# Moving five pieces of the shared network out of the expert loop, and a new order at the end of a mixture-of-experts kernel

## The chip, the cores and the metric

The kernel runs on one core of a Trainium2 chip. The metric is the time of one execution in microseconds (us); three runs of the kernel before are given, and their median counts. One further execution was taken by the hardware profiler, and every row shown here comes from it.

## The reference

The layer takes `x` (4, 512, 512) and `ctx` (4, 512, 128). First comes a graph attention of two layers. Its mask is the layernorm of `x`, multiplied by 1e10, so each row attends to one node alone: the kernel takes the position of each row's largest value instead of a softmax. Then a mixture of experts runs on the layernorm of the sum:

```python
x = x + xattn(ctx, layernorm(x), W0, ..., W1, ...)         # rows picked by argmax, twice
xf = layernorm(x).reshape(2048, 512)
scores = softmax(xf @ gate_w.T); topk_w, topk_idx = top_k(scores, 6)   # 64 experts, 128 rows each
gx = xp[buf_tok]                                            # (64, 128, 512), gathered
g, u = split(einsum('ech,ehi->eci', gx, gate_up_proj))      # 192 + 192
eo = einsum('eci,eih->ech', silu(g) * u, down_proj) * buf_w
routed = zeros.at[buf_tok].add(eo)                          # scattered with an addition
shared = silu(xf @ sh_gate.T) * (xf @ sh_up.T) @ sh_down.T  # 512 -> 384 -> 512, every row
out = x + routed + shared
```

All matrices are float32. The 2048 rows are 16 tiles of 128 rows (`NT`), in 4 groups of 4 tiles (`B`, `TB`).

## The kernel before, in words

Each engine has its own written-out queue (`block.sync`, `gpsimd`, `tensor`, `scalar`, `vector`), and semaphores join them. There are four stages.

**Attention**, up to about 95 us of the span. It fills `k.x`, one 128x512 tile per 128 rows.

**Routing**, up to about 154 us. TensorE makes the gate's logits (`gate`, `turn_logits`), VectorE picks the six experts (`choose`), TensorE counts places (`place`), VectorE makes one-hot matrices of the places (`split_high`, `split_low`, `split_rest`), TensorE turns them into lists of rows (`invert`, `collect`), and VectorE writes the list of each expert into `table` (L1283). GpSimd's gathers need this table. Four groups go through these steps one after the other.

**The expert loop** over `e` = 0 to 63. SyncE loads an expert's weights: `gu_w` (six buffers, `U`) for each expert, `dn_w` for each pair. GpSimd gathers the expert's rows into `gx`. TensorE transposes them (L811), multiplies by `gu_w` (L852), turns the hidden rows (L818) and, for pairs of experts, multiplies by `dn_w` (L827, L834, L837). ScalarE copies and takes silu, VectorE multiplies and writes `y` (L1337, eight buffers, `YB`), two experts at a time behind each odd `e`. GpSimd then scatters `y` with an addition into one of two sums in HBM, the lanes (L547): lane 0 is `out`, lane 1 is `odd_sum`. Within a lane each scatter waits until the one before has landed (`added`). Experts alternate between the lanes, except that the last `LAST` = 6 (58 to 63) all go to lane 0.

**Shared units** are woven in. The shared network is cut into 40 units, ten for each group of four tiles. The first six are `half_up` (L711, eight matmul records, 128x512; gate and up side of three slices `s` in turn), the last four are `shared_down` (L722, six records, one tile each). A `half_up` pair needs ScalarE's `silu` and VectorE's `shared_up` (L1214), and a `shared_down` VectorE's `shared_down` (L1220, adds to `k.x`, counts `x3_ready`). Units 0 to 4 (`EARLY` = 5) are in the routing stage, 32 to 39 (`LATE` = 8) behind the loop. The 27 between are spread by

```python
def first_unit(e):
    return EARLY + min(e * (units * B - EARLY - LATE) // (E - 2), units * B - EARLY - LATE)
```

**The end.** SyncE reads the two sums back by group (`load_sum(j, b)`, 1 MB each; lane 1 goes into the free `xnT` and, for the last group, into `y`; lane 0 into the free `gu_w`). VectorE adds them to `k.x` in `merge(j, b)` (L1370, four adds of one tile). SyncE stores each group when its tiles are complete (`store_out`, L352). `judge` computes a flag from bounds. After the block every engine loads the flag (`nc.values_load`) and, only if it is set, a general path would run; with these inputs it doesn't. `sent` is a semaphore which GpSimd raises behind the issue of scatters 62 and 63; VectorE waits for it before `merge(1, 0)` and before `shared_up(last, 1)`. SyncE's last instruction in the block waits for all stores (`out_stored`), ahead of the load of the flag.

Of the kernel before, what the change touches and what calls it, by code (L numbers as in the profile page):

```python
# [39 lines left out]
U = 6  # L40
# [3 lines left out]
LAST = 6  # L44
EARLY = 5
LATE = 8
# [29 lines left out]
def allocate(nc, ctx, k):  # L76
    def sb(name, shape, dt=F32):
        return ctx.enter_context(nc.sbuf_tensor(name, shape, dt))

    k.x = sb("x", [P, NT, D])  # L80
    k.ident = sb("ident", [P, P])
    k.ones = sb("ones", [P, P])
    k.flag = sb("flag", [1, 1], I32)
    k.gateT = sb("gateT", [P, KC, E])
    k.upT = sb("upT", [P, KC, 2 * SI])
    k.downT = sb("downT", [P, SC, D])
    k.mhalf = sb("mhalf", [P, NT])
    k.mv = sb("mv", [P, NT, 2])
    k.rstd = sb("rstd", [P, NT])
    k.tri = sb("tri", [P, P], F16)  # L90
    k.eighth = sb("eighth", [P, P], F16)
    k.strict = sb("strict", [P, P], F16)
    k.upto = sb("upto", [P, P], F16)
    k.pick_a = sb("pick_a", [P, (2 * SLO - 1) * SHI], F16)
    k.pick_z = sb("pick_z", [P, (2 * SLO - 1) * SHI], F16)
    k.same_e = sb("same_e", [P, 8])
    k.digit = sb("digit", [P, SHI], F16)
    k.token = sb("token", [P, NT])
    k.psum = [ctx.enter_context(nc.psum_tensor(f"bank{i}", [P, 512], F32)) for i in range(8)]


def main_block(nc, k, a):
# [3 lines left out]
    with ExitStack() as ctx:  # L106
# [140 lines left out]
        merged, total_ready, out_stored = (sem(s) for s in ("merged", "total_ready", "out_stored"))  # L247
# [46 lines left out]
        def first_unit(e):  # L294

            return EARLY + min(e * (units * B - EARLY - LATE) // (E - 2), units * B - EARLY - LATE)

# [22 lines left out]
        with nc.Block() as block:  # L320
            @block.sync
            def _(sp):
# [24 lines left out]
                def load_sum(j, b):  # L347
                    sp.dma_start(part_of(j, b), sums[j][b * N:(b + 1) * N, :].rearrange("(p t) d -> p t d", t=TB)).then_inc(sum_in[j][b], 16)

# [58 lines left out]
                for b in range(B - 1):  # L408
                    load_sum(1, b)
# [7 lines left out]
                for b in range(B):  # L417
                    store_out(b)
                sp.wait_ge(out_stored, 16 * B)

            @block.gpsimd
            def _(pool):
# [142 lines left out]
                for e in range(E):  # L565
                    scatter(e)
                    if e + GX < E:
                        gather(e + GX)
                    if e >= E - 2:
                        pool.sem_inc(sent, 1)  # L570
# [4 lines left out]
            def _(pe):  # L575
# [164 lines left out]
                for n in range(NT):  # L740
# [22 lines left out]
                    if n == 14:  # L763
                        turn_logits(0)
                xn_turn(6)
# [4 lines left out]
                unit(0)  # L770
# [5 lines left out]
                unit(1)  # L776
# [8 lines left out]
                unit(2)  # L785
                place(3)
                invert(2)
                pe.wait_ge(cross2_ready, 1)
                collect(RFIN, cross2, k.pick_z, lambda lo_: lo_).then_inc(spare_done, 1)
                unit(3)  # L790
# [3 lines left out]
                for u in range(4, EARLY):  # L794
                    unit(u)
# [75 lines left out]
            def _(act):  # L871
# [138 lines left out]
                gate_exp(1)  # L1010
                silu(0, 0)
                copy_logits(2)
# [3 lines left out]
                for t in range(TB):  # L1016
                    copy_xn(3 * TB + t)
                gate_exp(2)
# [3 lines left out]
                silu(0, 1)  # L1022
# [34 lines left out]
            def _(dve):  # L1057
# [158 lines left out]
                def shared_down(t):  # L1216
                    dve.wait_ge(sdn_done, t + 1)
                    if t >= NT - TB:
                        dve.wait_ge(merged, t + 1)
                    nc.vector.tensor_tensor(k.x[:, t, :], UP[t % 2][:], k.x[:, t, :], ALU.add).then_inc(x3_ready, 1)  # L1220
# [43 lines left out]
                split_low(1)  # L1264
                split_rest()
                shared_up(0, 0)
# [5 lines left out]
                cross_of(cross2, RTB, cross2_ready)  # L1272
                split_high(3)
# [3 lines left out]
                shared_up(0, 1)  # L1277
# [13 lines left out]
                link(nc.vector.tensor_tensor(gap[:], top[:, :, 0], top[:, :, 1], ALU.subtract))  # L1291

# [70 lines left out]
                def merge(j, b):  # L1363
                    dve.wait_ge(sum_in[j][b], 16)
                    for n in range(b * TB, (b + 1) * TB):
                        if j == 0 and b < B - 1:
                            dve.wait_ge(merged, n + 1)
                        elif j == 0 or b < B - 1:
                            dve.wait_ge(x3_ready, n + 1)
                        nc.vector.tensor_tensor(k.x[:, n, :], k.x[:, n, :], part_of(j, b)[:, n - b * TB, :],  # L1370
                                                ALU.add).then_inc((total_ready, merged)[j], 1)

                last = B - 1
                dve.wait_ge(sent, 1)
                merge(1, 0)
                dve.wait_ge(sent, 2)
                shared_up(last, 1)
                merge(1, last)
                merge(1, 1)
                shared_up(last, 2)  # L1380
                merge(1, 2)
                merge(0, 0)
                shared_down(last * TB)
                shared_down(last * TB + 1)
                merge(0, 1)
                shared_down(last * TB + 2)
                shared_down(last * TB + 3)
                merge(0, 2)
                merge(0, last)


def general_block(nc, k, a):


    with ExitStack() as ctx:
# [55 lines left out]
        for engine in (nc.vector, nc.scalar, nc.tensor, nc.gpsimd, nc.sync):  # L1451
            engine.sem_inc(g_passed, 1)
        stage(sync=load_weights, gpsimd=lambda: nc.gpsimd.memset(mhalf[:], -0.5))
# [85 lines left out]
def general_experts(nc, k, a):  # L1539


    with ExitStack() as ctx:
# [56 lines left out]
        with nc.Fori(0, NT) as n:  # L1599
# [16 lines left out]
            stage(vector=lambda: nc.vector.tensor_scalar(fits[:], bank[2][:, 0:E], SHI - 0.5, None, ALU.is_lt))  # L1616
# [54 lines left out]
def build(nc, a):  # L1671
    k = Kernel()
    with ExitStack() as ctx:
# [6 lines left out]
        nc.end_ifs()  # L1680

# [30 lines left out]
```

## Time and profile before

| | us |
|---|---|
| median of three runs | 596.72 (596.23 to 599.62) |
| the profiled execution, its own time | 597.44 |
| its span, first to last instruction | 595.6 |
| TensorE busy | 539.4 (91%) |
| VectorE busy | 246.1 (41%) |
| ScalarE busy | 161.7 (27%) |
| GpSimd busy | 225.1 (38%) |
| mean granted TensorE clock | 0.974 of full |

The span is 1.84 us shorter than the profiled execution's own time, and that execution is 0.72 us above the median. An engine's busy time says only how much work it has. Which wait ends last in a stage is read from the rows below.

### The profile page before, as it was taken

Reading aid. Unit: us, or ns where it says so; the run is one execution under the profiler, and the core shown is the slowest. Engines: PE = TensorE matmul, PEld = TensorE weight load, DVE = VectorE, ACT = ScalarE, POOL = GpSimd, SP = SyncE. Lnnn points to the kernel's source line nnn. Section 1 sums busy time; section 2 is a strip of 40 time slices with the busy share of each in tenths; the row PEclk is TensorE's granted clock in tenths of the full one; section 3 lists DMA queues with packets and bytes.
Section 4 is the critical chain, followed back from the end, with each engine's and each line's share of the span. In section 5 each row is a group of like instructions: output and inputs, shape, how many; then the busy total and the mean of one; then the engine's idle time right before and its main releaser. Section 6 shows DMA issues by size and latency. Waiting matters only on the chain.

```text
span 595.6 us, 6264 instructions
## 1 busy us (share of the span) xinstructions
PE 539.4 (91%) x2087; PEld 291.8 (49%) x2087; DVE 246.1 (41%) x641; ACT 161.7 (27%) x342; POOL 225.1 (38%) x221
## 2 busy tenths in 40 slices
PE   5999996676799999999999999999999999999490
PEld 2555543343355555555555555555555555554130
DVE  1885979999223222222123223222222223223473
ACT  4767787662111111211111111212111111210000
POOL 3052246632523543444334543444344434412300
PEclk9999999987999999999999999999999999999796
DMA  8956478795458999899988999999999999785486
GB/s 288 338 208 235 113 255 278 245 390 205 124 198 276 298 298 298 289 305 280 278 271 267 295 327 306 281 267 292 268 289 307 295 291 288 180 249 119 51 316 255
DMA packets 53559, 155.05 MB, mean 260 GB/s; under 512 B 7248, under 2 KB 8784, under 8 KB 51856
## 3 DMA queue, kind: packets, MB, share of 16 engines
q1 hardware_dynamic: 34800, 109.74, 50.8%
q0 software_dynamic: 16320, 40.39, 29.6%
q10 hardware_dynamic: 2400, 4.46, 2.2%
q8 instruction: 18, 0.29, 0.2%
q14 instruction: 21, 0.17, 0.1%
HBM read 116.28 MB, written 38.28 MB: 260 GB/s over the span
## 4 chain that ended last, share of the span: by engine, by line
PE 76%; DVE 11%; DMA 5%; issue 4%; ACT 2%; POOL 1%; DVEq 0%; SPq 0%; POOLq 0%; ACTq 0%
PE bank L852 29%; PE bank L711 11%; PE bank L722 7%; PE bank L837 6%; PE bank L811 5%; PE bank L827 5%; PE bank L834 5%; PE bank L624 5%; DMA out<-y,table 3%; PE bank L612 2%; PE bank L818 2%; DVE x L1109 1%; DVE bn L1112 1%; DMA w<-in_W 1%; DVE ones_hi L1174 1%
## 5 line engine op out<-in xcount | busy, mean ns | idle before, releaser
L852 PE MATMUL bank<-gu_w,gxT 128*128 128x384 f32 x512 | 178.9, 493 | 2.2 <-ACT gxT L1040 1.4
L547 POOL DMA_INDIRECT out<-y,table x35 | 55.8, 1593 | 213.4 <-DVE y L1337 194.6
L852 PEld LDWEIGHTS bank<-gu_w,gxT 128*128 128x128 f32 x512 | 93.3, 190 | 79.7 <-issue 28.8
L1048 ACT ACTIVATE eg<-bank 128x192 f32<-128x192 f32 x64 | 21.2, 332 | 287.6 <-PE bank L852 284.6
L711 PE MATMUL bank<-xnT,upT 128*128 128x512 f32 x192 | 90.5, 617 | 8.5 <-DVE shid L1214 8.5
L1323 DVE TENSOR_TENSOR hid<-bank,eg 128x192 f32<-128x192 f32 x64 | 22.9, 358 | 179.7 <-ACT eg L1048 164.1
L553 POOL DMA_INDIRECT gx<-rows_dram,table x64 | 63.3, 989 | 28.2 <-issue 19.2
L1337 DVE TENSOR_SCALAR y<-bank,gx 128x512 f32<-128x512 f32 x64 | 45.1, 746 | 60.3 <-PE bank L837 60.3
L711 PEld LDWEIGHTS bank<-xnT,upT 128*128 128x128 f32 x192 | 36.3, 198 | 47.2 <-issue 37.9
L624 PE MATMUL bank<-w,h1T 128*128 128x512 f32 x128 | 57.7, 593 | 0.0
L547 POOL DMA_INDIRECT odd_sum<-y,table x29 | 45.9, 1584 | 8.9 <-issue 8.9
L722 PE MATMUL bank<-downT,shid 128*128 128x512 f32 x96 | 43.7, 595 | 0.8 <-DVE shid L1214 0.8
L811 PEld LDWEIGHTS bank<-ident,gx 128*128 128x128 f32 x256 | 31.9, 141 | 22.3 <-issue 14.0
L1040 ACT ACTIVATE gxT<-bank 128x512 f32<-128x512 f32 x64 | 38.2, 597 | 8.3 <-PE bank L811 1.7
L811 PE MATMUL bank<-ident,gx 128*128 128x128 f32 x256 | 38.4, 273 | 1.7 <-DMA gx<-rows_dram,table 1.7
L624 PEld LDWEIGHTS bank<-w,h1T 128*128 128x128 f32 x128 | 23.9, 190 | 27.3 <-issue 25.7
L837 PE MATMUL bank<-dn_w,hidT 64*128 64x256 f32 x256 | 36.3, 402 | 0.0
L837 PEld LDWEIGHTS bank<-dn_w,hidT 64*128 64x128 f32 x256 | 22.0, 186 | 25.7 <-issue 24.3
L827 PE MATMUL bank<-dn_w,hidT 128*128 128x512 f32 x64 | 32.8, 594 | 0.6 <-DVE y L1337 0.6
L834 PE MATMUL bank<-dn_w,hidT 128*128 128x512 f32 x64 | 32.8, 594 | 0.0
L471 POOL DMA_INDIRECT node<-node_dram,node x16 | 16.4, 1025 | 29.3 <-DMA node_dram<-node 24.6
L722 PEld LDWEIGHTS bank<-downT,shid 128*128 128x128 f32 x96 | 17.1, 190 | 18.7 <-issue 16.3
(179 smaller groups left out, 512.8 us busy)
## 6 DMA issues: line engine op xcount, KB each, us to landing
gu_w<-in_gate_up SPq DMA_DIRECT2D x64, 768.0 KB, 6.5
dn_w<-in_down SPq DMA_DIRECT2D x32, 768.0 KB
x<-in_x SPq DMA_DIRECT2D x4, 1024.0 KB, 13.0
feat_dram<-feat SPq DMA_DIRECT2D x16, 256.0 KB, 4.0
out<-shid SPq DMA_DIRECT2D x8, 512.0 KB
odd_sum<-shid SPq DMA_DIRECT2D x8, 512.0 KB
rows_dram<-rows ACTq DMA_DIRECT2D x4, 1024.0 KB, 6.4
gu_w<-out SPq DMA_DIRECT2D x4, 1024.0 KB, 7.9
```

Of the source, the lines that this page charges most:

```text
L547: pool.indirect_dma_start(sums[lane(e)], bass.IndirectOffsetOnAxis(ap=table[:, e:e + 1], axis=0), y[:, e % YB, :], None, compute_op=ALU.ad ...
L553: pool.indirect_dma_start(gx[:, e % GX, :], None, a["rows_dram"][:, :], bass.IndirectOffsetOnAxis(ap=table[:, e:e + 1], axis=0)).then_inc( ...
L624: last = nc.tensor.matmul(L2[t % 2][:], h1T[:, b % 2, c, t * P:(t + 1) * P], w1[:, :, c, :], start=(c == 0), stop=(c == KC - 1))
L711: last = nc.tensor.matmul(UP[g][:], k.upT[:, c, g * SI + s * P:g * SI + (s + 1) * P], xnT[:, c, b * N:(b + 1) * N], start=(c == 0), stop=( ...
L722: last = nc.tensor.matmul(UP[t % 2][:], shid[b % 2][:, s, t * P:(t + 1) * P], k.downT[:, s, :], start=(s == 0), stop=(s == SC - 1))
L811: last = nc.tensor.transpose(GT[e % 2][:, c * P:(c + 1) * P], gx[:, e % GX, c * P:(c + 1) * P], k.ident[:])
L827: nc.tensor.matmul(DN[0][:], hidT[:, q % 2, 0, :], dn_w[:, q % UP2, 0, :], start=True, stop=False)
L834: nc.tensor.matmul(DN[1][:], hidT[:, q % 2, 2, :], dn_w[:, q % UP2, 2, :], start=True, stop=False)
L837: last = nc.tensor.matmul(DN[v][:, h * HALF:(h + 1) * HALF], hidT[v * REST:(v + 1) * REST, q % 2, 1, :], dn_w[v * REST:(v + 1) * REST, q % ...
L852: last = nc.tensor.matmul(GU[e % 2][:, 0:2 * I], gxT[:, e % 2, c, :], gu_w[:, e % U, c, :], start=(c == 0), stop=(c == KC - 1))
L1040: nc.scalar.activation(gxT[:, e % 2, :, :].rearrange("p c q -> p (c q)"), GT[e % 2][:], ACT.Copy).then_inc(gxT_ready, 1)
L1337: nc.vector.tensor_scalar(y[:, e % YB, :], DN[e % 2][:], gx[:, e % GX, D + e:D + e + 1], None, ALU.mult).then_inc(y_ready, 1)
```

## The change

Constants: `LAST` 6 to 4, `EARLY` 5 to 8, `LATE` 8 to 10. The 22 units in the loop are now spread over experts 0 to 56 (`E - U - 1` in place of `E - 2`), so the last seven have none. In the routing stage six units now stand ahead of the last `invert` where four stood, with `silu` and `shared_up` moved along, and 6 and 7 (two `shared_down`) follow the last `collect`, where unit 4 stood. Experts 58 and 59 go back to alternating lanes; `sent` now counts scatters 60 to 63, and SyncE, not VectorE, waits for it, between its loads of lane 1. The order on VectorE at the end is new, the last two tiles get their `shared_down` behind both merges, and the last group's store is split in two halves. The wait for the stores stands behind the load of the flag and the branch. One hunk is left out: it changes a constant in the general path, which isn't taken here.

```diff
@@ -41,9 +41,9 @@
 YB = 8
-LAST = 6
-EARLY = 5
-LATE = 8
+LAST = 4
+EARLY = 8
+LATE = 10
 EXP_FLOOR = -87.336
@@ -97,6 +97,8 @@
     k.psum = [ctx.enter_context(nc.psum_tensor(f"bank{i}", [P, 512], F32)) for i in range(8)]
+    k.out_stored = ctx.enter_context(nc.semaphore("out_stored"))
+    k.stores = 16 * (B + 1)
@@ -244,7 +246,7 @@
         sum_in = [[sem(f"sum{j}_in{b}") for b in range(B)] for j in range(2)]
-        merged, total_ready, out_stored = (sem(s) for s in ("merged", "total_ready", "out_stored"))
+        merged, total_ready, out_stored = sem("merged"), sem("total_ready"), k.out_stored
@@ -293,7 +295,7 @@
-            return EARLY + min(e * (units * B - EARLY - LATE) // (E - 2), units * B - EARLY - LATE)
+            return EARLY + min(e * (units * B - EARLY - LATE) // (E - U - 1), units * B - EARLY - LATE)
@@ -346,6 +348,16 @@
                     sp.dma_start(part_of(j, b), sums[j][b * N:(b + 1) * N, :].rearrange("(p t) d -> p t d", t=TB)).then_inc(sum_in[j][b], 16)
+
+                def store_last(h):
+
+                    here = slice(h * TB // 2, (h + 1) * TB // 2)
+                    if h == 0:
+                        sp.wait_ge(total_ready, NT - TB // 2)
+                    else:
+                        sp.wait_ge(x3_ready, NT)
+                    sp.dma_start(a["out"][(B - 1) * N:B * N, :].rearrange("(p t) d -> p t d", t=TB)[:, here, :],
+                                 k.x[:, (B - 1) * TB:B * TB, :][:, here, :]).then_inc(out_stored, 16)
@@ -405,8 +417,11 @@
                 sp.wait_ge(x3_ready, NT - TB)
-                for b in range(B - 1):
-                    load_sum(1, b)
+                load_sum(1, 0)
+                load_sum(1, 1)
+                sp.wait_ge(sent, 1)
+                load_sum(1, 2)
+                sp.wait_ge(sent, 2)
                 sp.wait_ge(y_ready, E - YB + TB)
@@ -414,9 +429,10 @@
                     load_sum(0, b)
-                for b in range(B):
+                for b in range(B - 1):
                     store_out(b)
-                sp.wait_ge(out_stored, 16 * B)
+                for h in range(2):
+                    store_last(h)
@@ -566,7 +582,7 @@
                         gather(e + GX)
-                    if e >= E - 2:
+                    if e >= E - LAST:
                         pool.sem_inc(sent, 1)
@@ -762,18 +778,19 @@
                         turn_logits(0)
+                unit(0)
                 xn_turn(6)
...
                 turn_logits(1)
-                unit(0)
+                unit(1)
                 for t in range(TB):
...
                 turn_logits(2)
-                unit(1)
+                unit(2)
                 invert(0)
@@ -782,16 +799,17 @@
                 invert_rest()
-                unit(2)
+                unit(3)
                 place(3)
+                unit(4)
                 invert(2)
...
                 collect(RFIN, cross2, k.pick_z, lambda lo_: lo_).then_inc(spare_done, 1)
-                unit(3)
+                unit(5)
                 invert(3)
...
                 collect(LIST, cross, k.pick_a, lambda lo_: SLO - 1 - lo_).then_inc(fin_done, 1)
-                for u in range(4, EARLY):
+                for u in range(6, EARLY):
                     unit(u)
@@ -1008,18 +1026,18 @@
                 gate_exp(1)
+                copy_logits(2)
                 silu(0, 0)
-                copy_logits(2)
                 store_rows(2)
...
                     copy_xn(3 * TB + t)
+                silu(0, 1)
                 gate_exp(2)
...
                 gate_exp(3)
-                silu(0, 1)
                 act.wait_ge(small_in, 80)
@@ -1215,8 +1233,10 @@
                     dve.wait_ge(sdn_done, t + 1)
-                    if t >= NT - TB:
-                        dve.wait_ge(merged, t + 1)
+                    if t >= NT - TB // 2:
+                        dve.wait_ge(total_ready, t + 1)
+                    elif t >= NT - TB:
+                        dve.wait_ge(merged, 2 * TB)
                     nc.vector.tensor_tensor(k.x[:, t, :], UP[t % 2][:], k.x[:, t, :], ALU.add).then_inc(x3_ready, 1)
@@ -1262,19 +1282,20 @@
                 split_low(1)
+                shared_up(0, 0)
                 split_rest()
-                shared_up(0, 0)
                 choose(3)
...
                 cross_of(cross2, RTB, cross2_ready)
+                shared_up(0, 1)
                 split_high(3)
...
                 nc.vector.tensor_copy(spare[:], POS[:, RFIN])
-                shared_up(0, 1)
+                shared_up(0, 2)
                 dve.wait_ge(tbl_done, B)
@@ -1289,6 +1310,8 @@
                 link(nc.vector.tensor_tensor(gap[:], top[:, :, 0], top[:, :, 1], ALU.subtract))
+                for u in range(2 * SC, EARLY):
+                    shared_down(u - 2 * SC)
@@ -1363,30 +1386,29 @@
                     for n in range(b * TB, (b + 1) * TB):
-                        if j == 0 and b < B - 1:
-                            dve.wait_ge(merged, n + 1)
+                        if j == 0 and not NT - TB <= n < NT - TB // 2:
+                            dve.wait_ge(merged, (1 + (0, 2, 3, 1)[b]) * TB)
                         elif j == 0 or b < B - 1:
...
                 last = B - 1
-                dve.wait_ge(sent, 1)
                 merge(1, 0)
-                dve.wait_ge(sent, 2)
-                shared_up(last, 1)
+                shared_up(last, 0)
                 merge(1, last)
                 merge(1, 1)
-                shared_up(last, 2)
+                shared_up(last, 1)
                 merge(1, 2)
                 merge(0, 0)
+                shared_up(last, 2)
+                merge(0, 1)
                 shared_down(last * TB)
+                merge(0, 2)
                 shared_down(last * TB + 1)
-                merge(0, 1)
+                merge(0, last)
                 shared_down(last * TB + 2)
                 shared_down(last * TB + 3)
-                merge(0, 2)
-                merge(0, last)
@@ -1450,6 +1472,7 @@
             engine.sem_inc(g_passed, 1)
+        stage(sync=lambda sp: sp.wait_ge(k.out_stored, k.stores))
         stage(sync=load_weights, gpsimd=lambda: nc.gpsimd.memset(mhalf[:], -0.5))
@@ -1678,6 +1701,7 @@
         nc.end_ifs()
+        nc.sync.wait_ge(k.out_stored, k.stores)
 # ---- launch: one core; inputs and outputs as the reference has them ----
```

## Rows read from the trace of the kernel before

**Rows 1.** Page, busy tenths of TensorE in 40 slices of 14.9 us.
```profile
PE   5999996676799999999999999999999999999490
```
**Rows 2.** Loop, busy time: PE, PEld, DVE, ACT, POOL, clock, DMA share, GB/s.
```profile
180.00:520.00 340.00, 340.00 (x1280) 188.46 (x1280) 88.88 (x188) 56.33 (x120) 145.93 (x113) 1.00 0.94 284
```
**Rows 3.** Waits of SyncE's DMA queue, 180 to 520 us: total, times, longest.
```profile
SPq L356 <- PE bank L852: 200.7, 54, 7.2
```
**Rows 4.** Chain that ended last, in the loop: start, us, piece.
```profile
499.78 2.58 PE bank L722 x6
...
504.28 2.78 PE bank L852 x8
...
511.70 3.44 PE bank L711 x8
...
517.05 2.78 PE bank L852 x8
```
**Rows 5.** Timeline of TensorE, routing: start, us, operation, idle time before.
```profile
98.55 1.10 PE L602 MATMUL bank<-ident,rows 128*128 128x128 f32 x8 [3.56 <-issue]
...
143.11 1.89 PE L680 MATMUL bank<-ones_lo,ones_hi 128*128 128x64 f16 x32 [4.62 <-DVE ones_lo L1186]
...
145.24 5.03 PE L711 MATMUL bank<-xnT,upT 128*128 128x512 f32 x8
...
157.64 0.63 PE L811 MATMUL bank<-ident,gx 128*128 128x128 f32 x4 [1.73 <-DMA gx<-rows_dram,table]
```
**Rows 6.** Timeline of VectorE, routing.
```profile
150.31 0.69 DVE L1214 TENSOR_TENSOR shid<-bank,sg 128x512 f32<-128x512 f32 x1 [0.62 <-PE bank L711]
```
**Rows 7.** Timeline of VectorE, behind the loop.
```profile
538.77 1.41 DVE L1337 TENSOR_SCALAR y<-bank,gx 128x512 f32<-128x512 f32 x2 [1.11 <-PE bank L837]
...
571.86 2.49 DVE L1370 TENSOR_TENSOR x<-x,gu_w 128x512 f32<-128x512 f32 x4
...
580.47 0.69 DVE L1220 TENSOR_TENSOR x<-bank,x 128x512 f32<-128x512 f32 x1 [1.72 <-PE bank L722]
```
**Rows 8.** Timeline of GpSimd, scatters of experts 58 to 63.
```profile
530.89 1.55 POOL L547 DMA_INDIRECT out<-y,table  x1 [9.32 <-DVE y L1337]
538.42 1.55 POOL L547 DMA_INDIRECT out<-y,table  x1 [5.97 <-DMA out<-y,table]
543.92 1.55 POOL L547 DMA_INDIRECT out<-y,table  x1 [3.95 <-DVE y L1337]
550.46 1.57 POOL L547 DMA_INDIRECT out<-y,table  x1 [4.99 <-DMA out<-y,table]
555.97 2.01 POOL L547 DMA_INDIRECT out<-y,table  x1 [3.95 <-DMA out<-y,table]
561.91 1.55 POOL L547 DMA_INDIRECT out<-y,table  x1 [3.92 <-DMA out<-y,table]
```
**Rows 9.** Timeline of SyncE's DMA issues, 505 to 596 us.
```profile
525.54 1.93 SPq L348 DMA_DIRECT2D xnT<-odd_sum  x3
543.24 0.35 SPq L348 DMA_DIRECT2D y<-odd_sum  x1
567.00 1.99 SPq L348 DMA_DIRECT2D gu_w<-out  x4
574.38 11.95 SPq L352 DMA_DIRECT2D out<-x  x4
```
**Rows 10.** Timeline of TensorE, behind the loop.
```profile
543.43 10.57 PE L711 MATMUL bank<-xnT,upT 128*128 128x512 f32 x24
562.48 6.33 PE L711 MATMUL bank<-xnT,upT 128*128 128x512 f32 x8 [8.48 <-DVE shid L1214]
569.59 10.83 PE L722 MATMUL bank<-downT,shid 128*128 128x512 f32 x24 [0.78 <-DVE shid L1214]
```
**Rows 11.** Busy time of a stretch behind the loop, columns as in rows 2.
```profile
562.48:568.10 5.62, 5.62 (x7) 2.40 (x8) 4.75 (x8) 0.00 (x0) 0.98 (x1) 0.53 0.49 63
```
**Rows 12.** Waits of SyncE's DMA queue, 560 to 600 us.
```profile
SPq L320 <- DMA out<-x: 3.9, 1, 3.9
```

More of the change, by code:

```diff
@@ L1615, in general_experts @@
             stage(tensor=lambda: products(bank[2][:, 0:E], [(k.tri[:], sel[:]), (k.eighth[:], seen[:])]))
-            stage(vector=lambda: nc.vector.tensor_scalar(fits[:], bank[2][:, 0:E], SHI - 0.5, None, ALU.is_lt))
+            stage(vector=lambda: nc.vector.tensor_scalar(fits[:], bank[2][:, 0:E], SHI - 0.5 - AWAY, None, ALU.is_lt))
             stage(vector=lambda: nc.vector.tensor_tensor(fits[:], fits[:], sel[:], ALU.mult))
```

## The prediction

> **What bounds the kernel now.** I read the page's slices first [rows 1]: TensorE is full nearly everywhere, with three thin places, in the routing stage (slices 7 to 11), behind the loop and at the very end. So I read three stretches apart.
>
> The loop: from 180 to 520 us TensorE is busy 340 of 340 us at full clock [rows 2]. The DMA share of 0.94 looks like a second bound. SyncE's queue says otherwise: its weight loads wait 54 times for TensorE to free a buffer, 200.7 us in total [rows 3]. The loads run as far ahead as six buffers allow, so TensorE sets the pace and the loop costs the sum of its matmuls. The chain of waits gives the prices: a `half_up` 3.44 us, a `shared_down` 2.58, and a pair of experts with one `half_up` lasts from 504.28 to 517.05, 12.77 us [rows 4], so a pair with no unit lasts 9.33.
>
> The routing stage: TensorE waits for VectorE or ScalarE, 3.56 us ahead of 98.55, 4.62 ahead of 143.11, and 1.73 for the first gathered rows ahead of 157.64 [rows 5]. Here VectorE is the engine in front.
>
> The end: the six scatters of one lane are issued at 530.89, 538.42, 543.92, 550.46, 555.97 and 561.91 [rows 8], each but the third and the first behind the landing of the one before (the third is named as waiting for `y`, but those rows were written from 538.77 on [rows 7], so it too had waited for a landing). The read of lane 0 starts at 567.00 [rows 9], 5.1 us behind the last issue. TensorE stands idle 8.48 us within this chain [rows 10], because `shared_up(3, 1)` on VectorE waits for `sent`. Then come merges, the last store's issue at 574.38 + 11.95 = 586.33 less its own 0.34, so 586.0 [rows 9], a wait of 3.9 us for it to land [rows 12], and about 5.4 us from its landing (590.2) to the end of the span at 595.6, in which flag and branch are handled.
>
> **The change part by part.** I work out each as a shift of the profiled execution.
>
> *Loop.* Units 5 to 31 were in it, now 8 to 29. Out go units 5, 30 and 31 (`half_up`) and 6 and 7 (`shared_down`): 3 x 3.44 + 2 x 2.58 = 15.5 us. Since TensorE never waits in the loop [rows 2], it all comes off, if nothing else turns up as a bound. Demand on the DMA engines rises little: 22 units over 57 experts instead of 27 over 62 make a pair 0.3 us shorter, and the last seven experts, without units, have their loads issued before. Dependent steps with no unit between them could stall; a pair has one unit at most in most places already, and the half of a pair without one runs through, so I take nothing.
>
> *Routing.* Added ahead of the table are units 4 and 5 and two `shared_up`. Unit 0 takes the 3.56 us idle ahead of 98.55, unit 4 the 4.62 us ahead of 143.11 [rows 5], each gap as long as the unit. Unit 5 takes the place of unit 3 at 145.24, which ran 5.03 us, at the half clock that follows the gap; with the gap filled I expect 3.6. VectorE has 0.7 us more in front of its last one-hot matrices, which the wait for the third `invert` absorbs, and it doesn't wait any longer for `half_up` (0.62 us ahead of 150.31 [rows 6]). That gives the table about 0.4 us earlier. Behind the last `collect`, units 6 and 7 cost 2 x 2.58 = 5.2, where unit 4 (3.44) and an idle 1.73 [rows 5] stood: also 5.2, so the first gather still covers them. Sum: -0.4 us, between -1.5 (all of the clock's loss returned) and +3.4 (one `half_up` uncovered). Loop and routing together: -15.9 us, so `y` of expert 60, from 538.77 [rows 7], comes at 522.9, and is ready 0.75 later.
>
> *Scatters.* Expert 59 goes to lane 1, so expert 60 waits only for 58, issued at 515 and long landed. Scatter 60 goes out at 523.9. Only three intervals follow, then the landing. SyncE's loads of lane 1 now start about here, 3 MB of them, as they started at 525.54 ahead of the scatter at 530.89, whose interval was 7.5 us; I take 7.5 for 60. The fourth load falls on scatter 61, as it fell on the one at 543.92 (6.5 us). Scatter 62 takes 5.7 (mean of 5.5, 5.5 and 5.9 [rows 8]) and the landing of 63 5.1. In all 24.8: lane 0 is complete at 548.7 instead of 567.0, -18.3 us. Bounds for this chain: 21.8 (four times 5.5) and 28 (7 on average).
>
> *The new wait on SyncE.* It waits for `sent` between loads of lane 1. Queued behind are the last two of these loads and nothing urgent; VectorE wants the fourth load at about 539. Nothing here ends last: 0 us.
>
> *TensorE behind the loop.* It ends the loop at 527 and runs units 30 to 35 till about 548.5, also under the scatters. 36 to 39 need `shared_up(3, 2)`, which on VectorE now stands behind `merge(0, 0)`. That is the price of the new order, and it replaces the old stall. The first read of lane 0 lands 4.86 us after its issue (567.00 to 571.86, where the merge starts [rows 7, 9]): 553.6. The merge takes 2.49, so `shared_up` starts at 556.1 and TensorE 0.75 later at 556.9, after 8.4 us idle. The row for such a case is the `half_up` at 562.48: after 8.48 us idle it took 6.33 us in place of 3.44 [rows 4, 10], and the granted clock of its stretch was 0.53, so 1.2 GHz nearly all through [rows 11]. It came back after 5.6 us of work. So four `shared_down` cost 4 x 2.58 = 10.3, plus half of 5.6 = 2.8, plus two waits of 0.8 for VectorE's additions, as the 0.78 at 569.59 [rows 10]: 571.6. VectorE's own work by then (merges 3 x 2.49, three additions) ends earlier, so TensorE is last. The final addition takes 0.7 [rows 7]: the last store goes out at 572.4, -13.6 us against 586.0.
>
> The Trainium skill (TensorE: Matmul & The Clock Gate, "Why this matters for your kernels") asks for no idle gaps between bursts of matmuls, because the clock falls back. That speaks against putting `shared_up(3, 2)` behind a merge, and the row at 562.48 agrees (6.33 us). A sum that ignored it would end 2.8 us earlier.
>
> *Last stores and flag.* The store's last part is 512 KB instead of 1 MB. With the wait behind the load of the flag, the 3.9 to 4.2 us of landing run beside the 5.4 us of flag and branch. Taken as fully hidden: 572.4 + 5.4 = 577.8. Bounds: 0 (hidden) and 4.2 us (the landing still first).
>
> **Sum.** Span 595.6 - 15.9 (loop, routing) - 2.4 (scatter chain beyond that) + 4.7 (four `shared_down` behind the merge, half clock) - 4.2 (stores beside the flag) = 577.8. The profiled execution lies 1.84 above its span and 0.72 above the median: 578.9, say 579.
>
> **Rivals.**
> *The DMA engines hold the loop.* For it: the share of 0.94 [rows 2]. Against: loads issued only as buffers come free [rows 3]. If the loop kept its pace, the 15.5 us would be lost: 594.4, within 1% of before. Chance 0.07, and 0.05 for a loss of part of it, 585 to 591.
> *Clock and chain go well.* TensorE keeps full clock (-2.8), or the first scatters aren't slowed by the loads (-3.0): 573 to 577. Chance 0.22.
> *The landing isn't hidden,* or a `half_up` in routing is not covered: 582 to 587. Chance 0.18.
> *Slower: the shared units go in front of the table.* VectorE's queue is in order, and `shared_up(0, 1)` and `(0, 2)` now stand ahead of the work that writes the table. If those gaps aren't usable, units 3 to 5 run there at the half clock (3 x 5.03 [rows 5]) and 6 and 7 too (2 x 5.16), 25.4 us, where 5.2 are spent now: +20.2 and no 0.4 gained, so 599.5. It turns the sign once the first product by expert weights, now 1.4 us behind the transposes of 157.64, comes later than 177. The gaps of rows 5 speak against it. Chance 0.03, together with whatever else goes that far.
> *The end doesn't get shorter than the loop does,* say because scatters still chain at 7 us: this is within the range.
>
> **How the numbers follow.** Forecast (577 to 582) 0.45, clock and chain 0.22, landing or routing 0.18, DMA 0.12, slower 0.03. The range of 573 to 587 leaves out about 0.17. A measurement of this kernel tells about 1% from no change, so 590.8 and 602.7 are the bounds: faster 0.91, same 0.07, slower 0.02.
>
> **What would show it.** The last loop matmul near 527; pairs of experts without a unit at 9.3 us; the first L811 of the loop near 157.2; only four scatters in the last chain, the first near 524, intervals 7.5, 6.5, 5.7; the reads of lane 0 near 549; six `half_up` on TensorE without the 8.48 us gap, then a gap of about 8 us ahead of the four `shared_down`, of which the first take 5 us; the last store near 572 and the end 5.4 us behind it. A loop with idle TensorE and waits for `gu_w` would prove the first rival, and a first L811 beyond 160 the last.

## The result, and the profile after

The changed kernel takes 583.19 us in the median of four runs (581.39 to 583.66), against 597.05 before (the three runs above and one more): 0.9757 of it, interval 0.973 to 0.9785. Its profiled execution took 581.39 with a span of 579.8; the prediction had 577.8 for the span and 579 for the time. The measured time lies in its range of 573 to 587, but 1.2 us above the stretch of 577 to 582 that it called its forecast.

The loop first. Busy time by stretch of the changed kernel, and the waits of SyncE's queue from 160 to 500 us:

```profile
180.00:500.00 320.00, 320.00 (x1218) 178.28 (x1217) 83.89 (x180) 54.66 (x116) 141.62 (x111) 1.00 0.97 296
```
```profile
SPq L368 <- PE bank L870: 250.3, 58, 36.8
```
TensorE is still busy all the time and the loads still wait for it, though the DMA share rose from 0.94 to 0.97 and the rate from 284 to 296 GB/s [rows 2, 3]. Now TensorE's timeline in the routing stage and behind the loop:

```profile
95.33 1.04 PE L618 MATMUL bank<-ident,rows 128*128 128x128 f32 x8
96.21 3.60 PE L727 MATMUL bank<-xnT,upT 128*128 128x512 f32 x8
...
143.53 1.11 PE L696 MATMUL bank<-ones_lo,ones_hi 128*128 128x64 f16 x32 [0.75 <-DVE ones_lo L1204]
144.47 0.40 PE L713 MATMUL bank<-cross,pick_z 128*128 128x64 f16 x8
144.79 3.70 PE L727 MATMUL bank<-xnT,upT 128*128 128x512 f32 x8
...
152.14 5.40 PE L738 MATMUL bank<-downT,shid 128*128 128x512 f32 x12
157.56 0.63 PE L829 MATMUL bank<-ident,gx 128*128 128x128 f32 x4
...
527.15 0.60 PE L818 MATMUL bank<-ident,rowstat 128*1 128x128 f32 x4
...
560.75 12.07 PE L738 MATMUL bank<-downT,shid 128*128 128x512 f32 x24 [11.55 <-DVE shid L1232]
```
The gaps of rows 5 are filled: 4.62 us became 0.75, the `half_up` behind it takes 3.70 us instead of 5.03, and the two `shared_down` end where the gathered rows arrive. The loop (first transposes to the statistics behind its last product) runs from 157.56 to 527.15, 369.6 us. Before it was 157.64 to 542.68 (the statistics, 0.75 us ahead of the `half_up` at 543.43 [rows 10]), 385.0: the difference is 15.45. This length hardly varies: it is 369.57 us in the traces of `last6` and `woven` below, and 385.04 in `before_late_wait`.

Behind it stands the chain of scatters (GpSimd's timeline) and the reads and stores that follow (SyncE's issues):

```profile
524.27 1.55 POOL L563 DMA_INDIRECT out<-y,table  x1 [5.50 <-DVE y L1360]
534.02 1.57 POOL L563 DMA_INDIRECT out<-y,table  x1 [8.21 <-DMA out<-y,table]
541.96 1.91 POOL L563 DMA_INDIRECT out<-y,table  x1 [6.37 <-DMA out<-y,table]
547.84 1.55 POOL L563 DMA_INDIRECT out<-y,table  x1 [3.97 <-DMA out<-y,table]
```
```profile
522.38 2.22 SPq L350 DMA_DIRECT2D xnT<-odd_sum  x3
533.84 0.35 SPq L350 DMA_DIRECT2D y<-odd_sum  x1
552.79 1.98 SPq L350 DMA_DIRECT2D gu_w<-out  x4
560.12 8.47 SPq L364 DMA_DIRECT2D out<-x  x3
570.06 3.85 SPq L359 DMA_DIRECT2D out<-x  x2
```
Four scatters are left in the last chain, against the six of rows 8: 59 now goes to the other lane, and 58 is issued long before 60 has its rows. But the first two intervals are 9.75 and 7.94 us. Lane 0 is read from 552.79, 14.2 us earlier than before [rows 9], though the loop ended 15.5 us earlier. The last store is issued at 570.06 + 3.85 - 0.34 = 573.6, 20.8 us behind the start of that read (19.0 before), and the span ends 6.2 us behind it (9.6 before).

### The profile page after: what moved, and what is told of

It reads as the page before. It is cut to its first block, busy times and chain, and to the rows that moved or that the text cites. A ratio compares the mean times of both kernels' runs of the same rounds, so it can differ in the third digit from the quotient of the medians.

```text
span 579.8 us, 6266 instructions
## 1 busy us (share of the span) xinstructions
PE 536.4 (93%) x2087; PEld 290.6 (50%) x2087; DVE 245.3 (42%) x641; ACT 161.8 (28%) x342; POOL 224.6 (39%) x221
## 4 chain that ended last, share of the span: by engine, by line
PE 57%; DMA 18%; DVE 10%; issue 8%; SPq 2%; ACT 2%; POOL 2%; POOLq 0%; DVEq 0%; ACTq 0%
PE bank L870 22%; DMA out<-y,table 12%; PE bank L727 7%; PE bank L738 6%; PE bank L855 4%; PE bank L829 4%; PE bank L640 4%; PE bank L852 3%; PE bank L845 3%; DMA raw_down<-in_sh_down 3%; DMA odd_sum<-y,table 3%; DVE bn L1130 1%; DVE x L1127 1%; PE bank L836 1%; DVE ones_hi L1192 1%
## 5 line engine op out<-in xcount | busy, mean ns | idle before, releaser
L563 POOL DMA_INDIRECT out<-y,table x34 | 54.1, 1591 | 199.6 <-DVE y L1360 166.2
L727 PE MATMUL bank<-xnT,upT 128*128 128x512 f32 x192 | 86.2, 595 | 1.6 <-ACT sg L973 1.5
L738 PE MATMUL bank<-downT,shid 128*128 128x512 f32 x96 | 44.9, 611 | 11.6 <-DVE shid L1232 11.6
L727 PEld LDWEIGHTS bank<-xnT,upT 128*128 128x128 f32 x192 | 34.9, 190 | 39.1 <-issue 36.4
L563 POOL DMA_INDIRECT odd_sum<-y,table x30 | 47.5, 1582 | 9.1 <-issue 9.1
```

The costliest lines, as they stand in the source:

```text
L563: pool.indirect_dma_start(sums[lane(e)], bass.IndirectOffsetOnAxis(ap=table[:, e:e + 1], axis=0), y[:, e % YB, :], None, compute_op=ALU.ad ...
L727: last = nc.tensor.matmul(UP[g][:], k.upT[:, c, g * SI + s * P:g * SI + (s + 1) * P], xnT[:, c, b * N:(b + 1) * N], start=(c == 0), stop=( ...
L738: last = nc.tensor.matmul(UP[t % 2][:], shid[b % 2][:, s, t * P:(t + 1) * P], k.downT[:, s, :], start=(s == 0), stop=(s == SC - 1))
```

## The experiments

All but `before_late_wait` are edits of the changed kernel. Ratios are to the kernel before; times are medians.

**Two units back into the loop** (`early6`)
```diff
-EARLY = 8
+EARLY = 6
```


> The changed kernel with EARLY = 6, so units 6 and 7 (two shared_down) go back from the place behind the last collect into the loop. Theory (TensorE paces the loop, and the wait for the first gathered rows covers the two units): the first transposes of the loop stay near 157.5 us, TensorE idle ahead of them is 5 us or so again, and everything from the loop's end on is 2 x 2.58 = 5.2 us later, span near 585. Rival (the DMA engines pace the loop): the loop's end hardly moves, under 1.5 us.

590.07 us, 0.9876 (0.985 to 0.9903), span 587.9. The first transposes and the stretch behind them:
```profile
157.96 1.09 PE L829 MATMUL bank<-ident,gx 128*128 128x128 f32 x4 [5.28 <-DMA gx<-rows_dram,table]
...
167.97 0.60 PE L829 MATMUL bank<-ident,gx 128*128 128x128 f32 x4
```
```profile
157.90:168.00 10.10, 8.48 (x25) 5.04 (x26) 0.36 (x1) 1.52 (x3) 7.68 (x6) 0.76 0.83 248
```
TensorE idles 5.28 us, so the two units had cost nothing there in the changed kernel's trace. In its trace the same transposes as those of 167.97 stand at
```profile
165.65 0.60 PE L829 MATMUL bank<-ident,gx 128*128 128x128 f32 x4
```
The loop of `early6` starts 0.4 us later, is 2.3 us behind at this place, and ends (start of the statistics) at 534.62, 7.5 us behind. So 5.2 us are the two units, and 1.9 come from the clock, which was low behind the gap (mean 0.76 over 157.9 to 168, against 1.00). Filling the gap also kept the clock. The rival, a loop paced by DMA, is out.

The two units are not always free. In four of the later traces, whose routing stage has the same code, TensorE's clock is low under them. In `woven` its mean is 0.64 from 152.22 to 157.00, against 1.00 from 152.14 to 157.50 in the changed kernel:
```profile
152.22 7.09 PE L738 MATMUL bank<-downT,shid 128*128 128x512 f32 x12
159.15 0.60 PE L829 MATMUL bank<-ident,gx 128*128 128x128 f32 x4
```
They take 7.09 us there (also in `last6` and `quarter_reads`, and 6.85 in `as_it_lands`) instead of 5.40, and the first transposes wait for them and no longer for the rows: about 1.5 us are lost, an estimate from 7.09 - 5.40 less the little slack.

**Two units from behind the loop into it** (`late8`)
```diff
-LATE = 10
+LATE = 8
...
-                shared_up(last, 0)
```


> The changed kernel with LATE = 8 and VectorE's shared_up(3, 0) in the loop again, so units 30 and 31 (two half_up) go back from behind the loop into it. Theory (work behind the loop is hidden by the chain of scatters): all of 2 x 3.44 = 6.9 us comes back, span near 586.7, and TensorE's gap ahead of the last four shared_down grows from 11.6 to 18 us. Rival (late units cost as much there as in the loop): within 1.5 us of the changed kernel.

589.75 us, 0.9873 (0.9847 to 0.9898), span 586.8, +7.0. The loop lasts 376.47 us, 6.88 more, which is two `half_up`. Units behind the loop are free, as long as the scatters take longer. The idle time that I expected as one gap of 18 us comes as two:
```profile
534.54 10.57 PE L727 MATMUL bank<-xnT,upT 128*128 128x512 f32 x24
552.15 6.20 PE L727 MATMUL bank<-xnT,upT 128*128 128x512 f32 x8 [7.04 <-DVE shid L1232]
567.23 12.36 PE L738 MATMUL bank<-downT,shid 128*128 128x512 f32 x24 [8.88 <-DVE shid L1232]
```

**The lanes as before** (`last6`)
```diff
-LAST = 4
+LAST = 6
```


> The changed kernel with LAST = 6: scatters 58 to 63 in one lane again. Theory (the chain of scatters is what the end waits for): scatter 59 joins the chain ahead of 60, so the first interval comes before 60 and the read of lane 0 is later by 3 to 5 us (a further interval of 5.7 to 7.5 us, less the time that 60 now waits for y), span near 584. Lane 1 is read earlier, at about 513 to 516, which shortens the interval behind 60 by up to 3 us and could bring the sum down to +1. Rival (the lane change is hidden): within 1 us.

583.38 us, 0.9764 (0.9738 to 0.979): the same as the changed kernel. GpSimd's timeline:
```profile
516.38 1.55 POOL L563 DMA_INDIRECT out<-y,table  x1 [5.89 <-DVE y L1360]
525.76 1.55 POOL L563 DMA_INDIRECT out<-y,table  x1 [7.83 <-DVE y L1360]
531.18 1.55 POOL L563 DMA_INDIRECT out<-y,table  x1 [3.87 <-DMA out<-y,table]
537.81 1.62 POOL L563 DMA_INDIRECT out<-y,table  x1 [5.07 <-DMA out<-y,table]
543.33 1.56 POOL L563 DMA_INDIRECT out<-y,table  x1 [3.90 <-DMA out<-y,table]
548.91 1.55 POOL L563 DMA_INDIRECT out<-y,table  x1 [4.01 <-DMA out<-y,table]
```
The chain has one interval more, because 59 is in it. But lane 1 is complete earlier, so its three reads start at 514.6 and slow only scatter 58 (9.4 us). That costs little: in the changed kernel too 8.9 us pass from scatter 58 (515.36) to scatter 60 (524.27), which waits for `y`. The next intervals are 5.4, 6.6, 5.5 and 5.6. The read of lane 0 starts at 553.70, 0.9 us later than in the changed kernel, with a loop that ended 1.0 us later: no difference. The rival holds: what the shorter chain gains is lost again, because the reads then fall on scatters that count.

**Reads of lane 1 cut to a quarter** (`quarter_reads`; three quarters of that sum are left out)
```diff
-                    sp.dma_start(part_of(j, b), sums[j]...
+                    w = slice(0, 1 if j else TB)
+                    sp.dma_start(part_of(j, b)[:, w, :], sums[j]...[:, w, :]).then_inc(sum_in[j][b], 16)
```


> The changed kernel, in which each of the four reads of lane 1 brings 256 KB instead of 1 MB (three quarters of the lane 1 sum are left out of the result). Measured in the changed kernel: intervals between the last scatters 9.75, 7.94, 5.88 and 4.95 us to the read of lane 0. Theory (the reads of lane 1 slow the scatters that run beside them): the first two fall to 6 to 6.5 us each, the read of lane 0 starts 4.5 to 5.5 us earlier, span near 575. Rival (an accumulating scatter is that slow by itself so soon behind the loop): intervals stay within 0.7 us, span within 1 us.

577.0 us, 0.967 (0.9643 to 0.9697), span 575.0. GpSimd's timeline:
```profile
524.28 1.55 POOL L564 DMA_INDIRECT out<-y,table  x1 [5.50 <-DVE y L1361]
530.21 1.57 POOL L564 DMA_INDIRECT out<-y,table  x1 [4.38 <-DMA out<-y,table]
535.85 1.96 POOL L564 DMA_INDIRECT out<-y,table  x1 [4.07 <-DMA out<-y,table]
541.77 1.55 POOL L564 DMA_INDIRECT out<-y,table  x1 [3.96 <-DMA out<-y,table]
```
The intervals are 5.93 and 5.64 us in place of 9.75 and 7.94: the reads cost the chain 6.1 us. The theory holds. The span gains only 4.8 of them, and TensorE's timeline shows where the rest went:
```profile
554.57 13.47 PE L739 MATMUL bank<-downT,shid 128*128 128x512 f32 x24 [5.79 <-DVE shid L1233]
```
The pause ahead of the four `shared_down` is half as long as in the changed kernel, 5.79 us, but they take 13.47 us, not 12.07.

**Twelve idle matmuls in the gap** (`fill`)
```diff
                 for u in range(units * B - LATE, units * B):
                     unit(u)
+                    if u == units * B - 5:
+                        for q in range(3):
+                            for c in range(KC):
+                                nc.tensor.matmul(bank[6][:], k.upT[:, c, 0:P], xnT[:, c, 0:N], start=(c == 0), stop=(c == KC - 1))
```


> The changed kernel with twelve matmuls more on TensorE behind unit 35 (three times a half_up, 10.3 us, into a bank that nobody reads), in the gap of 11.55 us ahead of the last four shared_down. Theory (the gap costs the clock): granted clock 1.00 there, the four shared_down take 10.3 to 11 us instead of 12.07 and the end comes 1.2 to 2.8 us earlier, as far as VectorE isn't then the last (its own merges would end 1 us earlier at most without waits: so 1 to 1.5 is likelier). Rival (the clock is no part of it): no difference, or later by what the extra work overlaps.

579.24 us, 0.9703 (0.9689 to 0.9717), span 578.4. TensorE's timeline, then the stretch behind the gap with the fill, and last the same of the changed kernel:
```profile
560.55 10.57 PE L738 MATMUL bank<-downT,shid 128*128 128x512 f32 x24 [1.20 <-DVE shid L1237]
```
```profile
560.50:565.00 4.50, 4.45 (x11) 2.06 (x12) 3.97 (x7) 0.00 (x0) 0.00 (x0) 1.00 1.01 322
```
```profile
560.75:565.00 4.25, 4.25 (x7) 1.96 (x8) 2.35 (x4) 0.00 (x0) 0.00 (x0) 0.64 1.00 332
```
Work that nobody reads keeps 2.4 GHz, the four `shared_down` take 10.57 us in place of 12.07, and the last store goes out 1.7 us earlier. So the gap's cost by the clock is 1.5 us in this place. The time is 3.9 us below the changed kernel's, more than the clock explains: the medians of the spans differ by 2.4 us (577.4 and 579.8), and the rest lies around the span.

**`shared_up(3, 2)` ahead of the merge** (`up_first`)
```diff
+                shared_up(last, 2)
                 merge(0, 0)
-                shared_up(last, 2)
                 merge(0, 1)
```


> The changed kernel with VectorE's shared_up(3, 2) ahead of merge(0, 0) instead of behind it. TensorE can then run units 36 and 37 under the scatters, by 555, but 38 needs shared_down(12), which stands behind merge(0, 1), near 563. Theory (the idle gap costs the clock): TensorE is idle again for 8 us ahead of 38, so 38 and 39 run at the half clock, 5.1 us each in place of 2.58, and the last store moves by less than 1.5 us. Rival (only order and work count): the last store goes out as soon as VectorE has done its merges, 3 us earlier, span near 576.8.

580.6 us, 0.9727 (0.9714 to 0.9741), span 577.0. The last store is 18.4 us behind the read of lane 0, not 20.8: -2.4, so more than I gave it. TensorE was idle before the last two `shared_down` as expected (7.57 us), but only two `shared_down` are left behind it: they take 7.25 us (5.42 at full clock; the mean clock of 562 to 569 us was 0.74), where four took 12.07.

**All four `shared_down` under the scatters** (`woven`)
```diff
+                shared_up(last, 2)
+                shared_down(last * TB)
+                shared_down(last * TB + 1)
                 merge(0, 0)
+                shared_down(last * TB + 2)
+                shared_down(last * TB + 3)
+                for b in range(1, B):
+                    merge(0, b)
```
(The rest of the old order goes; tiles 12 to 15 wait for `merged` alone, the last half store for `total_ready`.)

> The changed kernel with shared_up(3, 2) and the shared_down of tiles 12 and 13 ahead of merge(0, 0), those of 14 and 15 right behind it, and the last store waiting for the last merge. TensorE's four shared_down then run from 549 to 560 without a gap. Theory (behind the read of lane 0 only VectorE's adds have to follow): merge(0, 0) starts at 557.6 as now, then 16 adds of 0.61 and two of 0.6 end near 568.7 instead of 573.6, if the last read of lane 0 has landed by 566: span near 575, -4.5 to -5. Rival (the reads of lane 0, 4 MB, end last): adds of group 3 wait for the read, -2 to -3.

579.68 us, 0.9707 (0.9688 to 0.9727), span 579.1. The last store is issued 15.9 us behind the read of lane 0 (554.02), 4.9 us sooner than in the changed kernel, but the end comes 9.2 us behind it. SyncE's waits show why; the changed kernel has no such row:
```profile
SPq L1701 <- DMA out<-x: 6.8, 1, 6.8
```
The wait for the stores behind the branch now ends last. DMA rates of `woven` and of the changed kernel from 553 us on (GB/s, 40 slices of 0.65 and 0.67 us) show the queues busy till about 576 in either, at about 400 GB/s in most slices:
```profile
GB/s 73 0 36 158 243 449 413 388 449 413 449 413 425 437 401 425 303 328 206 303 401 400 461 437 425 413 413 449 449 413 388 401 419 413 249 61 61 36 36 24
```
```profile
GB/s 0 170 243 364 413 437 486 388 413 401 449 473 388 388 316 243 303 218 352 461 437 425 388 425 473 425 425 388 425 407 394 267 407 249 61 12 0 0 12 36
```

**The same with quarter stores of groups 0 to 2** (`woven_quarter_stores`; the rest of these groups is not stored)

> The kernel called woven (last store issued at 569.9, 15.9 us behind the start of the read of lane 0, but the span's end 9.2 us later instead of 6.2), in which the stores of groups 0 to 2 bring only 256 KB each instead of 1 MB (the rest of the result isn't stored). Theory (4 MB read and 4 MB stored behind the last scatter end last, whatever the order of the adds): with 2.25 MB less the span ends 15.9 + 6.2 = 22.1 us behind the start of the read of lane 0, near 576 for a start near 554; rival (the end is fixed by flag and branch, which were late by chance): 25 us behind it as in woven, near 579.

575.72 us, 0.9662 (0.963 to 0.9693), span 574.1: 22.2 us behind its read of lane 0 (551.92) against 25.1 in `woven`, as the theory said. Behind the scatters 4 MB are read and 4 MB stored, and this traffic is nearly as long as the adds.

**The wait for the stores, by itself** (`wait_in_block`, and `before_late_wait`, the kernel before with nothing but the wait moved)
```diff
                 for h in range(2):
                     store_last(h)
+                sp.wait_ge(out_stored, k.stores)
```


> The changed kernel with the wait for the stores as SyncE's last instruction inside the block again, ahead of the load of the flag (the wait behind the branch stays, already met). Theory (landing of the last half store and flag run side by side): span longer by the landing, about 3 us for 512 KB (4.2 us for 1 MB in the kernel before), less the 0.8 us by which the end now takes longer than 5.4: +2.5 to +3.5. Rival (the landing still ends last): no difference, under 0.5 us.

> The kernel before with nothing changed but the wait for the stores, which stands behind the load of the flag and the branch. Theory of the prediction: the span gets shorter by the landing of the last store, 3.5 to 4.2 us, and so does the time, 593 us. Rival (what lies around the span is longer by as much, as 581.39 to 583.66 us for spans of 579.4 to 581.6 in the changed kernel hint): the span is shorter by 2 to 4 us, the time by less than 1.

The first: 583.25 us, 0.9767 (0.9737 to 0.9798), span 581.7, the end 8.4 us behind the last store's issue. SyncE waits less for a store of 512 KB than for one of 1 MB (3.9 [rows 12]):
```profile
SPq L322 <- DMA out<-x: 2.7, 1, 2.7
```
The span shows +1.9 us, the time nothing that the interval could tell. The second: 595.13 us, 0.9969 (0.9952 to 0.9986), so 1.9 us (0.8 to 2.9). The span's median is 2.5 us shorter (592.45 against 594.95, 12 and 16 runs), and what lies around it 0.6 longer (3.1 against 2.5). Both theories missed part: the gain is real, but half of what I took.

**Lanes alternating up to expert 61** (`last2`)
```diff
-LAST = 4
+LAST = 2
```


> The changed kernel with LAST = 2: experts 60 and 61 alternate too, lane 0 ends with 62 and 63. What stretched the last chain are the reads of lane 1 beside scatters 60 and 61 (9.75 and 7.94 us; 5.9 and 5.6 with quarter reads). Theory: scatters 60 and 61 go out together at 524 to 526 before any read of lane 1 starts, 62 near 530, 63 (beside the reads) near 538, and the read of lane 0 starts at 545 to 547 instead of 552.8, although lane 1 is read 10 us later; the end follows it, span 573 to 575. Rival (the reads of lane 1, issued later, now end last through merge(1, 3), merge(1, 1) and unit 35): TensorE's last half_up ends near 554 and the gain is at most 3 us.

580.84 us, 0.9735 (0.9714 to 0.9756), span 577.4. Lane 0 is read from 543.29, 9.5 us earlier, as expected or better. But VectorE works through its queue in order:
```profile
548.85 2.50 DVE L1393 TENSOR_TENSOR x<-x,y 128x512 f32<-128x512 f32 x4 [6.49 <-DMA y<-odd_sum]
```
`merge(1, 3)` waits for the last read of lane 1 with everything behind it. The rival was right: -2.4.

**VectorE's order as the inputs land** (`as_it_lands`, with `LAST = 2` and without SyncE's waits for `sent`)
```diff
+                shared_up(last, 0)
                 merge(1, 0)
-                shared_up(last, 0)
-                merge(1, last)
-                merge(1, 1)
                 shared_up(last, 1)
+                merge(1, 1)
                 merge(1, 2)
+                shared_up(last, 2)
+                merge(1, last)
+                for b in range(B):
+                    if b < 2:
+                        shared_down(last * TB + b)
+                    merge(0, b)
+                    if 0 < b < last:
+                        shared_down(last * TB + b + 1)
```
(The rest of the old order goes; tiles 12 to 15 wait for lane 1's merges alone, the last half store for `total_ready`.)

> LAST = 2 as in last2 (where the read of lane 0 started at 543.3, 9.5 us earlier than in the changed kernel, but only 2.4 us of it reached the span, because merge(1, 3) waited until 548.9 with everything queued behind it), and VectorE's queue in the order in which its inputs come: shared_up(3, 0) before any merge, lane 1's groups 0, 1, 2 and then 3, shared_up(3, 2) ahead of merge(1, 3), the four shared_down between lane 0's merges; SyncE doesn't wait for sent between the reads of lane 1. Theory (order on VectorE held the end, then the 12 MB of reads and stores and its 43 operations): merge(0, 0) starts at 552 to 553, last store issued at 563 to 565 instead of 573.6, its landing about 3 us later, span 569 to 572. Rival (DMA traffic alone sets the end, at the 340 to 360 GB/s seen behind the last scatter): 8.4 MB from 543.3 on, with the rest of lane 1, end near 570 to 573, span 574 or more.

574.28 us, 0.9609 (0.9592 to 0.9627), span 571.9. The dropped waits moved little: lane 1 is read from 532.37 and 534.53, in `last2` from 531.31 and 534.79. VectorE's timeline and SyncE's issues:
```profile
550.36 2.48 DVE L1389 TENSOR_TENSOR x<-x,y 128x512 f32<-128x512 f32 x4
...
553.98 2.48 DVE L1389 TENSOR_TENSOR x<-x,gu_w 128x512 f32<-128x512 f32 x4
...
563.00 2.48 DVE L1389 TENSOR_TENSOR x<-x,gu_w 128x512 f32<-128x512 f32 x4
```
```profile
544.43 1.77 SPq L350 DMA_DIRECT2D gu_w<-out  x4
...
564.31 1.54 SPq L359 DMA_DIRECT2D out<-x  x2
```
The last store goes out at 565.5, 8.1 us earlier than in the changed kernel. From 549.76 on VectorE idles only 0.53 us. This version is faster than the changed kernel (0.9757) and than `last2` (0.9735).

## Why the prediction was right, and where its sizes were off

*Loop, -15.5.* Measured: 15.45, from the first transposes to the statistics. Demand on the DMA engines rose and changed nothing. `early6` and `late8` give the same price per unit (5.2 for two `shared_down`, 6.88 for two `half_up`).

*Routing, -0.4 (-1.5 to +3.4).* From the transposes ahead of unit 0 (start 93.95 before, 95.33 after) to the first gathered rows it took 63.7 us before and 62.2 after, so -1.5, the lower bound; the clock kept by the filled gap (3.70 in place of 5.03) is part of it. One trace of each doesn't settle this term: with two units behind the last `collect` the same stretch took 62.2 to 64.8 us in ten later traces, and 62.8 in `before_late_wait`. The stage ahead was 1.4 us longer in the profiled execution (95.33 in place of 93.95), which hid the gain: `y` of expert 60 was written at 523.24, predicted 522.9. That it fits so well is luck, since traces with the same loop put it between 522.3 (`up_first`) and 524.8 (`woven`).

*Scatter chain, 24.8 us.* This term failed, by 3.7: 28.5 from scatter 60 to the read of lane 0. I took 7.5 and 6.5 for the first two intervals; they were 9.75 and 7.94. It also lies outside the bounds that the prediction gave it (21.8 to 28; the lower should be 22.0, four times 5.5). The prices came from rows where the reads had started 5.3 us ahead of the scatter [rows 8, 9]; now they start 1.9 us ahead. `quarter_reads` shows that the reads are the cause (5.93 and 5.64 without most of them). That their start so close to the scatter makes them dearer is argued from the rows: 9.4 us with 1.8 us ahead in `last6`, against 7.5 with 5.3. The first two intervals together are 17.7 us here and 17.3 to 17.7 in seven later traces with the same lanes and full reads. With that the "-2.4 for the scatter chain" was +1.3, and `last6` shows that the change of lanes brought nothing.

*Four `shared_down` behind the merge, 23.7 us from the read of lane 0 to the last store.* It was 20.8. The mechanism was right: the gap, 11.55 us, and a clock of 0.64 behind it. But the clock cost less than the 2.8 us that I had copied from rows 11, and the two waits of 0.8 didn't come: 12.07 us where I had 14.7. `fill` prices the clock at 1.5 us. A single row was too little for this term: the four `shared_down` cost 13.47 us, so 2.9 for the clock, in `quarter_reads`. The new order's other cost is larger: `woven` saves 4.9 us to the last store.

*Stores beside the flag, -4.2.* Another term that was mis-sized. From the last store's issue to the end of the span 9.6 us became 6.2, so -3.4. Of this 2.2 belong to the moved wait (8.4 in `wait_in_block`) and 1.2 to the half store, which lands sooner (a wait of 2.7 in place of 3.9). The kernel before with the wait moved gained 1.9 us in time. What handles flag and branch takes 6.2 us from the last issue on, and 6.2 to 7.2 in the later traces in which the stores aren't waited for first, where 5.4 had followed the landing.

*Around the span.* I took the 1.84 and 0.72 of one execution. In the changed kernel's four runs time and span differ by 1.6, 3.5, 2.1 and 3.7 us. So of the 4.3 us between forecast and median 2.0 are the span's (+4.1 chain and `y`, -2.9 `shared_down`, +0.8 end) and 2.3 this difference. In the other kernels' runs it lies anywhere from 1.3 to 4.3 us, and no run explains it. It stays open. That the span came out within 2.0 us is luck in part: the chain's error and that of the `shared_down` are larger and have opposite signs.

*Rivals.* The DMA-paced loop is excluded by 320 of 320 us busy and by `early6`. The slower one, units in front of the table, by 157.56. "Landing or routing" has the measured time in its band, 582 to 587, but not for its reason: what of the landing was not hidden is 0.8 us of the 4.3. "Clock and chain go well" came half true, the clock cheaper by 1.3 us and the chain dearer. The last one held as to the scatters: they chain at 7.1 us on average, and the read of lane 0 moved less (14.2 us) than the loop's end (15.5).

## What to carry to other kernels

Work moved from a saturated stretch into an engine's idle gaps was worth its full duration here (15.45 us of 15.5), as long as the gap was the longer of the two, and a gap filled on TensorE returned some clock besides (1.9 us in `early6`, 1.5 in `fill`). At an end made of serial small DMAs, ask what bulk transfers start beside them: taking one scatter out of the chain brought nothing, because the large reads then fell on its first links. And put an in-order queue into the order in which its inputs land: with that, and with the `shared_down` woven between the merges, the same lanes gave 6.6 us more (`last2` to `as_it_lands`).

## What the hardware showed that I hadn't expected

From the issue of a serial accumulating scatter of 128 rows x 2 KB to the next issue it takes 5.4 to 6.0 us alone, and 9.4 to 10.6 with 3 MB of reads started within the 2 us before it.

What a pause of TensorE costs the work behind it doesn't follow from its length. After 8.5 us the same `half_up` took 6.33 us in the kernel before [rows 10] and 5.54 in `before_late_wait`:
```profile
561.75 5.54 PE L711 MATMUL bank<-xnT,upT 128*128 128x512 f32 x8 [8.50 <-DVE shid L1214]
```
Four `shared_down` took 13.47 us after 5.79 us (`quarter_reads`), but 12.01 to 12.65 after pauses of 11.5 to 11.8 (`wait_in_block`, the changed kernel, `last6`, `early6`), and 10.57 with the gap filled. A pause of 5.28 us ahead of the loop cost 1.9 us (`early6`).
Moving a wait behind a branch changed the span by 1.9 to 2.5 us but the time by about 1.9 in one kernel and by nothing measurable in the other.
